# Attention and mixture-of-experts block on one core: a division without reciprocals, hidden tiles turned by DMA, down products three units late

## The reference

```python
def step(carry, kv_t):                     # over the 128 positions, per channel
    p, q, o = carry; kt, vt = kv_t
    no = maximum(o, u + kt); A = exp(o - no); E = exp(u + kt - no)
    y = (A * p + E * vt) / (A * q + E)
    no2 = maximum(w + o, kt); A2 = exp(w + o - no2); E2 = exp(kt - no2)
    return (A2 * p + E2 * vt, A2 * q + E2, no2), y
x = x + wkv(w, u, layernorm(x), ctx)       # k = layernorm(x), v = ctx
h = layernorm(x)
comb = top-2 of softmax(h @ gate_w.T), scattered to 8 columns
moe = sum_e comb[:, e] * ((silu(h @ eg[e].T) * (h @ eu[e].T)) @ ed[e].T)
sh  = sigmoid(h @ s_gate.T) * ((silu(h @ sg.T) * (h @ su.T)) @ sd.T)
out = x + moe + sh
```

## Time and profile before

| | us |
|---|---|
| median of 3 timed runs | 566.74 |
| lowest and highest of them | 566.08 and 566.8 |
| the profiled execution, whole | 566.06 |
| its span, first to last instruction | 564.3 |

### The profile page before, as it was taken

How to read it: one execution, slowest core, us unless ns; L and a number is a source line. 1 busy time by engine, 2 the same in 40 slices (tenths; PEclk the granted TensorE clock), 3 DMA queues, 4 the chain that set the end, 5 groups by cost and what they waited for, 6 DMA issues and landing times.

```text
span 564.3 us, 10142 instructions
## 1 busy us (share of the span) xinstructions
PE 486.2 (86%) x2671; PEld 258.5 (46%) x2671; DVE 421.3 (75%) x954; ACT 275.9 (49%) x534; POOL 345.4 (61%) x422
## 2 busy tenths in 40 slices
PE   1116789899999999999999979999999999999970
PEld 1113345345455555454555435445545555555530
DVE  5678987899989899999898867566656656666650
ACT  4848837575573864765837333433333333333310
POOL 5767956857948669588486364334375565555332
PEclk9999989999999999999999999999999999999995
DMA  7970105105213223151101320315576776677453
GB/s 283 415 271 19 38 19 187 57 21 188 76 46 143 77 82 143 38 188 62 52 20 39 105 88 15 113 45 102 101 122 117 141 119 116 110 131 123 69 73 38
DMA packets 25929, 59.14 MB, mean 105 GB/s; under 512 B 6314, under 2 KB 6314, under 8 KB 24338
## 3 DMA queue, kind: packets, MB, share of 16 engines
q0 software_dynamic: 9824, 20.90, 21.3%
q1 hardware_dynamic: 16050, 37.59, 18.5%
HBM read 37.83 MB, written 20.65 MB: 104 GB/s over the span
## 4 chain that ended last, share of the span: by engine, by line
PE 52%; POOL 17%; issue 10%; DVE 9%; DMA 7%; ACT 3%; SPq 1%; POOLq 0%; DVEq 0%; ACTq 0%
PE GU L884 28%; PE DN L899 14%; DMA out<-wall,idsa 5%; POOL wall L445 4%; PE XT L829 3%; PE HT L829 3%; POOL yb L429 2%; POOL nrm L411 2%; POOL nrm L413 2%; DVE wall L1071 2%; POOL wall L424 2%; POOL wall L421 2%; DVE wall L1078 1%; PE YT L829 1%; SPq L366 1%
## 5 line engine op out<-in xcount | busy, mean ns | idle before, releaser
L884 PE MATMUL GU<-wall,xt 128*128 128x512 f16 x768 | 187.0, 384 | 2.1 <-DVE wall L1173 2.0
L899 PE MATMUL DN<-wall,hx 128*128 128x512 f16 (+1 forms) x618 | 150.8, 380 | 7.2 <-DVE hx L1200 4.5
L884 PEld LDWEIGHTS GU<-wall,xt 128*128 128x128 f16 x768 | 74.8, 99 | 70.4 <-issue 3.7
L584 POOL DMA_INDIRECT out<-wall,idsa x39 | 62.0, 1590 | 73.1 <-SPq L370 35.1
L659 ACT ACTIVATE hx<-HT 128x256 f16<-128x256 f32 x103 | 39.0, 379 | 127.4 <-PE HT L829 110.6
L899 PEld LDWEIGHTS DN<-wall,hx 128*128 128x128 f16 x618 | 60.4, 98 | 81.9 <-issue 6.0
L1200 DVE TENSOR_TENSOR hx<-HT,hx 128x256 f16<-128x256 f32 x103 | 43.1, 418 | 64.3 <-ACT hx L659 59.7
L654 ACT ACTIVATE th<-GU,scl 128x256 f32<-128x256 f32 x103 | 48.5, 471 | 80.0 <-PE GU L884 76.1
L884 PE MATMUL GU<-wall,kb 128*128 x240 | 61.4, 379 | 0.2 <-DVE kb L1374 0.2
L884 PE MATMUL GU<-wall,xnb 128*128 x228 | 58.5, 379 | 0.6 <-DVE xnb L1374 0.6
L574 POOL DMA_INDIRECT xb<-xn_rows,idsi x39 | 40.2, 1030 | 30.5 <-DMA out<-xb 16.3
(11 more groups left out here) (163 smaller groups left out, 747.3 us busy)
## 6 DMA issues: line engine op xcount, KB each, us to landing
wall<-wgu SPq DMA_DIRECT2D x12, 1024.0 KB, 9.7
wall<-wd SPq DMA_DIRECT2D x12, 512.0 KB, 10.3
out<-xb SPq DMA_DIRECT2D x20, 256.0 KB
xb<-x SPq DMA_DIRECT2D x16, 256.0 KB, 2.7
cb<-ctx_t SPq DMA_DIRECT2D x16, 256.0 KB
xn_rows<-xnb SPq DMA_DIRECT2D x16, 256.0 KB
xb<-xn_rows,idsi POOLq DMA_INDIRECT x39
out<-wall,idsa POOLq DMA_INDIRECT x39
```

The costliest lines, as they stand in the source:

```text
L584: pool.indirect_dma_start(out, bass.IndirectOffsetOnAxis(ap=idsa[:, j:j + 1], axis=0), ye[j % RESULTS], None, compute_op=ALU.add).then_inc ...
L884: ins = nc.tensor.matmul(GU[par][:], lhs(xp, c), gate_up(base, wp, c), start=m == 0, stop=m == 3 * HC - 1)
L899: ins = nc.tensor.matmul(DN[:], hx[par][:, hp * IE + c * P:hp * IE + (c + 1) * P], down(base, wp, c), start=start and m == 0, stop=stop an ...
```

## The change

It has these parts:

- For tiles 3 to 15 (DIV = 3) the quotient is made without reciprocals. ScalarE takes an Exp of the denominator's bits read as an integer (`guess`), which is near the reciprocal; GpSimd multiplies denominator and numerator by it (`trial`); ScalarE takes two Squares (`correction`); VectorE multiplies in two passes (`divide`). The transposes YT of tile i move from the end of turn i to behind the first unit of turn i + 1.
- For the shared units the f32 transposes are gone. ScalarE and VectorE make the f16 halves of the hidden tile as it is, in hr (two buffers), and SP turns it into hx (three buffers, HX) by a DMA transpose of 128x512 f16. Routed units keep the f32 transposes, in the bank YT. The bank HT is named HB and holds one of the two hidden tiles.
- Down products come three units after their gate products, where they came two after. `accumulate` moves later in VectorE's order, `hidden_t` of the last routed unit moves ahead of the last down products, and GpSimd adds rows one slot later beside its gathers.
- Expert weights come in six DMAs of 256 KB, spread between the DMA transposes over two turns.
- The sums of squares of an expert are one matmul of four columns where they were two of two; VectorE adds them up.
- Some small index arrays move into space of a buffer that is free by then.

```diff
+HX = 3
+PIECES = 6
+DIV = LAG + 1
...
-        hb = [sb(f"hb{i}", [P, IE]) for i in range(2)]
-        hx = [sb(f"hx{i}", [P, 2 * IE], F16) for i in range(2)]
+        hb1 = sb("hb1", [P, IE])
+        hr = [sb(f"hr{i}", [P, 2 * IE], F16) for i in range(2)]
+        hx = [sb(f"hx{i}", [P, 2 * IE], F16) for i in range(HX)]
...
-        HT, DN = bank("HT"), bank("DN")
+        HB, DN = bank("HB"), bank("DN")
+        hb = [HB[:, 0:IE], hb1[:, :]]
+        hb_routed = [by_time[:, 0:IE], hb1[:, :]]
...
+            def turn_hidden(n):
+                sp.wait_ge(h_lo, n + 1)
+                wait_from(sp, dn, n - HX + 1)
+                sp.dma_start(hx[n % HX][:, :].rearrange("p (c t) -> p c t", t=P), hr[n % 2][:],
+                             transpose=True).then_inc(h_turned[n % HX], 16)
...
             def turn(i, j, sq_e, hi_e, ws_e, lo_e):
...
+                if j > 0:
+                    turn_hidden(n - 1)
+                if i == LAG:
+                    load_x(i + 3)
+                if i > LAG + 1 and i + 2 < B:
+                    load_x(i + 2)
+                if i < B - 1:
                     load_ctx(i + 1)
...
+                piece(0)
+                turn_hidden(n)
+                piece(1)
+                turn_hidden(n + 1)
+                store_xn(i - 1)
+                piece(2)
+                turn_hidden(n + 2)
+                if j > 0:
                     store_sum(j - 1)
...
+            def trial(t):
+                pool.wait_ge(guessed, t - DIV + 1)
+                nc.gpsimd.tensor_tensor(wkv(t, 2), wkv(t, 2), wkv(t, 0), ALU.mult).then_inc(tried, 1)
+                nc.gpsimd.tensor_tensor(wkv(t, 3), wkv(t, 3), wkv(t, 0), ALU.mult).then_inc(ymul, 1)
...
                 norm(i - 1, 1, agg2, norm2, xn_rdy)
                 if i == LAG:
                     shared_d_lo(1)
+                if i + 2 < B:
+                    norm(i + 2, 0, agg1, norm1, k_rdy)
+                if i >= DIV:
+                    trial(i)
                 if lo_e is not None:
                     expert_lo(lo_e, 2)
                 if ws_e:
                     expert_lo(ws_e, 0)
-                if i + 2 < B:
-                    norm(i + 2, 0, agg1, norm1, k_rdy)
...
-                quotient(i)
+                if i < DIV:
+                    quotient(i)
...
             for j in range(GATHERS, NSLOT):
                 gather_tile(j)
-                add_rows(j - GATHERS)
+                if j > GATHERS:
+                    add_rows(j - GATHERS - 1)
...
             def unit_hi(n, par):
...
+                act.wait_ge(h_rdy, n + 1)
+                if n >= 2:
+                    act.wait_ge(h_turned[(n - 2) % HX], 16 * ((n - 2) // HX + 1))
+                nc.scalar.activation(hr[par][:, 0:IE], hb[par], ACT.Copy).then_inc(h_hi, 1)
+
+            def guess(t):
+                act.wait_ge(nd, t + 1)
+                nc.scalar.activation(wkv(t, 0), wkv(t, 2).bitcast(I32), ACT.Exp, bias=divc[:, 0:1],
+                                     scale=GUESS_SCALE).then_inc(guessed, 1)
+
+            def correction(t):
+                act.wait_ge(tried, t - DIV + 1)
+                nc.scalar.activation(wkv(t, 1), wkv(t, 2), ACT.Square, bias=divc[:, 1:2],
+                                     scale=DIV_SCALE).then_inc(corrected, 1)
+                nc.scalar.activation(wkv(t, 2), wkv(t, 2), ACT.Square, bias=divc[:, 2:3],
+                                     scale=DIV_SCALE).then_inc(corrected, 1)
...
                 router_out(i - 2)
+                if i >= DIV:
+                    guess(i)
...
                 if i + 2 < B:
                     first_norm(i + 2)
+                if i >= DIV:
+                    correction(i)
                 unit_hi(n + 2, 0)
...
-                nc.tensor.matmul(LG[:, 0:2], ones[:], ssqe[:, 0:2], start=True, stop=False)
-                nc.tensor.matmul(LG[:, 0:2], ones[:], ssqe[:, 2:4], start=False, stop=True).then_inc(sq_sum, 1)
+                nc.tensor.matmul(LG[:, 0:4], ones[:], ssqe[:], start=True, stop=True).then_inc(sq_sum, 1)
...
                 if before is not None:
-                    down_products(n - 2, par, *before)
-                if not (isinstance(n, int) and n == 0):
-                    hidden_t(n - 1, 1 - par)
+                    down_products(n - HX, *before)
+                if n > N_EXP:
+                    hidden_t(n - 1)
...
                         router(i - 2, 2 + sum(a < i for a in SQUARED_IN))
+                        if i > LAG:
+                            y_back(i - 1)
                         if i + 1 < B:
                             keys_t(i + 1)
...
-                y_back(i)
...
-            down_products(n - 2, n % 2, base_of[NSLOT - 2], True, True, B + NSLOT - 2)
-            hidden_t(n - 1, (n - 1) % 2)
-            down_products(n - 1, (n - 1) % 2, base_of[NSLOT - 1], True, True, B + NSLOT - 1)
+            hidden_t(N_EXP + NSLOT - 1)
+            for j in range(NSLOT - HX, NSLOT):
+                down_products(N_EXP + j, base_of[j], True, True, B + j)
...
+            def divide(t):
+                dve.wait_ge(ymul, t + 1)
+                dve.wait_ge(corrected, (t - DIV) * 2 + 2)
+                STT(wkv(t, 3), wkv(t, 1), DIV_ADD[0], wkv(t, 3), ALU.add, ALU.mult).then_inc(half_div, 1)
+                dve.wait_ge(half_div, t - DIV + 1)
+                dve.wait_ge(y_t, t)
+                STT(grid(yb[:])[:, :, 1:T], grid(wkv(t, 2))[:, :, 1:T], DIV_ADD[1], grid(wkv(t, 3))[:, :, 1:T], ALU.add,
+                    ALU.mult).then_inc(y_rdy, 1)
...
                 hidden_lo(n + 2, 0)
+                if i >= DIV:
+                    divide(i)
                 hidden(n + 3, 1, SHARED)
...
-                if j == 1:
+                if j == HX - 1:
                     accumulate(B - 1)
-                if j >= 2:
-                    expert_rows(j - 2)
+                if j >= HX:
+                    expert_rows(j - HX)
                 hidden(N_EXP + j, r, expert_at[j])
```

More of the change, by code:

```diff
@@ L175, in build @@
         r_cmp, r_eid, r_row, r_one, r_of = taken(NSLOT * E), taken(NSLOT), taken(E), taken(E), taken(2)
+        eidi, idsi, idsa, wsl, pad_of = (taken(NSLOT) for _ in range(5))
+        eidi, idsi, idsa, before_i = (a.bitcast(I32) for a in (eidi, idsi, idsa, taken(RESULTS * NSLOT)))
         ids_back, ids_float = by_time[0:NSLOT, 0:P * LW].bitcast(I32), yb[0:NSLOT, 0:P]
@@ L328, in _ @@
             load_expert(0)
-            def turn(i, j, sq_e, hi_e, ws_e, lo_e):
-                if 0 < i < B - 1:
-                    load_ctx(i + 1)
-                if i == 1:
-                    load_expert(1)
-                if i + 1 in SQUARED_IN[2:]:
-                    load_expert(squares_of(i + 1))
-                if i > 0:
-                    store_xn(i - 1)
-                if j is not None and j > 0:
+            for i in range(LAG):
+                if i > 0:
+                    load_ctx(i + 1)
+                    load_expert(1)
+                    store_xn(i - 1)
+                load_x(i + 3)
@@ L340, in turn @@
                     store_sum(j - 1)
-                if i + 3 < B:
-                    load_x(i + 3)
                 if i == B - 1:
                     store_probs(0, 0, PART)
-            turns(turn)
+            turns(turn, LAG)
+            n = SU * (B - LAG)
+            turn_hidden(n - 1)
             sp.wait_ge(y_rdy, B)
-            load_expert(E - 1)
+            sp.wait_ge(y_first, B - DIV)
+            load_expert(E - 1, 0, 3)
+            turn_hidden(n)
             store_xn(B - 1)
+            load_expert(E - 1, 3, 6)
@@ L351, in _ @@
+            turn_hidden(n + 1)
+            turn_hidden(n + 2)
             store_sum(B - LAG - 1)
+            turn_hidden(n + 3)
             store_probs(1, PART, B)
-            for j in range(B - LAG, B - 1):
-                store_sum(j)
+            for u in range(3):
+                turn_hidden(n + SU + u)
+            store_sum(B - 2)
+            turn_hidden(N_EXP - 1)
             store_sum(B - 1)
@@ L391, in other_consts @@
             def other_consts():
+                for k, value in enumerate((GUESS_BIAS, *DIV_BIAS)):
+                    link(pool.memset(divc[:, k:k + 1], value))
                 link(pool.memset(all16[:], 1.0))
@@ L590, in _ @@
                 gather_tile(j)
[L591 to L592 removed]
+                if j > GATHERS:
+                    add_rows(j - GATHERS - 1)
+            for j in range(NSLOT - GATHERS - 1, NSLOT):
                 add_rows(j)
@@ L1282, in turn @@
                     keys(i + 1)
-                reciprocals(i, 1, 2)
+                if i < DIV:
+                    reciprocals(i, 1, 1)
+                if later:
+                    accumulate(j - 1)
+                if i < DIV:
+                    reciprocals(i, 2, 1)
                 hidden_lo(n + 1, 1)
-                reciprocals(i, 3, 1)
+                if i < DIV:
+                    reciprocals(i, 3, 1)
                 hidden(n + 2, 0, SHARED)
@@ L1389, in _ @@
```

(5 more changed lines are left out.)

122 lines of the change are left out of this document (73 added, 49 removed).

## The result

The changed kernel takes **576.22 us** (median of 4 runs, 574.28 to 578.52) beside 566.77 (566.08 to 567.41) of the kernel before: ratio 1.017, 95% interval 1.012 to 1.021. It is slower by some 9.5 us. The forecast was 549.2, the range 544 to 568.

A forecast was written before the change was run, and what follows sets the result against it. The prediction took TensorE, busy 98% of the shared expert's turns, as the bound, with VectorE almost as full. Gains of 23.4 us less losses of 6.5 gave net 16.9: 566.06 - 16.9 = 549.2 us, range 544 to 568.

The forecast's parts named there:

- Hidden transposes, their DMAs: Shared units: dropping TensorE's f32 transposes gains 12.6 us; the DMA transposes replacing them land in 3.5 us, unseen.
- the second estimate: DMA transposes of hidden tiles: 5.2 us each, from the Trainium skill's 1309 ns per 128x128 block; kernel some 650 us.
- Rival 3: Slower: in the turns the transposes hold the DMA engines or land late; 567 to 620 us, chance 0.18.
- The waits at YT, HT and for low halves (6.2): TensorE's waits in the turns at these three places go, gaining 6.2 us.
- the price of the new waits: In the turns, XT comes late through GpSimd's longer queue: 0.15 us a turn taken, 2 us lost.
- VectorE's share falls to some 80% of a shorter turn: In the turns the division takes 2.3 us off VectorE, which lets TensorE keep its gain.
- Rival 2: A ring of the side engines sets the turn, giving back 4 to 12 us: 553 to 562 us, chance 0.22.
- Start: At the kernel's start, some TensorE waits for YT, HT and down products leave: 0 to 6 us gained, 3 taken.
- Tail: At the kernel's end, slot 36's rows are weighed later, behind the last hidden transposes: 4.1 us lost.
- Gather of slot 5: The gather of slot 5's rows goes out later behind accumulate(15) and lands late: 0.4 us lost (0 to 2.5).
- Sum: Whole kernel: 23.4 us gained, 6.5 lost, net 16.9, giving 549.2 us.

The follow-up runs named there:

- e7: The changed kernel with GpSimd's low halves of experts 1 to 6 cut to 8 columns, that part of the result left out: 547.28 us.
- e1: The changed kernel with the division undone: all 16 tiles take the four reciprocals and GpSimd's one product: 561.14 us.
- e12: The kernel before with the division without reciprocals alone, hidden tiles still turned on TensorE, YT at the turn's end: 582.33 us.
- e6: The changed kernel with both untransposed hidden tiles of the shared units in the PSUM bank HB: 573.5 us.
- e9: e6 with GpSimd's norm of the tile put ahead of the second low half of the expert's weights: 572.5 us.
- e11: e7 with seven more products of 8 columns after each cut product, and both hidden tiles in PSUM: 560.28 us.
- e10: The changed kernel with the reciprocals back, both hidden tiles in PSUM and GpSimd's norm ahead of the second low half: 550.65 us.
- e14: The changed kernel with VectorE's small steps moved from ahead of the divide to the turn's end: 594.61 us.
- e8: The changed kernel with reciprocals back and both hidden tiles in PSUM, each DMA transpose done twice, the second after the first lands: 624.38 us.

## Why the prediction was wrong, step by step

- **Hidden transposes, their DMAs**: right. The landing was taken as 3.5 us (5.2 in the second estimate) and is 2.4 at the median; nothing in the changed kernel waits for it. e7's two turns, 35.29 us, are inside 35.0 to 35.4. Rival 3 had the time of the result but not its cause; e1 and e7, with all transposes, are faster than before.
- **The waits at YT, HT and for low halves (6.2)**: right only in e7. In the changed kernel YT waits 8.2, for VectorE now.
- **The step that failed: the price of the new waits, "between 0 and 0.9 us a turn; I take 0.15"**, as the sum has it (2.0 us). Two turns take 40.2 us where 35.0 to 35.4 were forecast, 2.5 us more a turn, nearly three times the upper bound; over the twelve tiles it is the 27 us by which e7 is ahead. TensorE waits 26 us, at XT, GU and YT. The working took each duration from a row and let it stand. But VectorE's durations depend on what GpSimd does beside it, and GpSimd's on VectorE. In the turn shown, the small steps meet three products instead of one and wait 2.8 us, on a ring of in-order queues. The earlier trace rows could not show the price: before, that ring had slack behind TensorE. The trace of before did have the sign of it, 366 ns as the mean for a step that takes 0.16 us at its shortest.
- **"VectorE's share falls to some 80% of a shorter turn"** failed as well, and its sum is off: 92% of 18.9 us less 2.3 are 15.2 us, 80% of the old turn but 86% of one of 17.6. It came to 89% of a longer turn. Yet it did not decide: e7 has the forecast turn with VectorE at 93%, and e12 loses 17 us with VectorE at 82%.
- **Rival 2** (a ring of the side engines) is nearest to what happened; its price, 4 to 12 us given back, was too small: 27 came. It counted GpSimd's busy time and not what GpSimd and VectorE do to each other. Its shares (nearly 90% for GpSimd) did not come either: the ring closes with every engine below 90%.
- **Start**: 3 us taken, 5.7 measured, near the bound of 6. **Tail**: 4.1 forecast; the rows of slot 36 start 3.63 us after the last tanh (552.76 and 549.13) where they started 0.27 ahead of it, 3.9. **Gather of slot 5**: TensorE waits 0.9 us for it, 0.4 was taken.
- **Sum**: forecast 549.2; e7 is at 547.3. That the sum comes so near is in part luck: the start gave 2.7 us more than was taken, and the small terms were not measured one by one. The 29 us from there to the changed kernel come with GpSimd's wide low halves, 7 of them with reciprocals too.

What stays open: how the 22 us of interaction divide between stretched steps and held queues. e6 gives 3 us and e9 1 more, at a lower clock; e11 lies 13 us from e6 and from e7, but changes the phase as well. They don't add to a full account. The best kernel that computes everything is e10, with the reciprocals, the tile in PSUM and the norm first: 550.65, 2.5% less than before (0.970 to 0.979), some 14 us.

## What to carry to other kernels

Before moving work from one kind of instruction to another on VectorE, look at what GpSimd runs beside it, and at the mean against the shortest duration of the smallest steps of both: the step over 16 columns had a mean of 366 ns and a shortest of 160 in the kernel before, so it was waiting, though it counts as busy. An engine that is freed brings nothing if its work lies on a ring of in-order queues; walk the chain of the new order once around and put every wait and every stretched step on it. And moving the stretched steps away, as in e14, can cost more than they do, if another queue waits for them.

## What the runs showed of the hardware

- A VectorE instruction whose operands lie in SBUF can last as long as the GpSimd product that runs when it starts (0.85, 1.25 and 1.18 us for steps of 0.15), the product itself keeping its 1.27; a pass of 0.68 that starts with 0.88 of a product left takes 1.43. Putting one of the operands in PSUM brought 888 ns back to 396 and the kernel 6 us.
- The later one waits on GpSimd too: its products on f32 tiles take 1.45 to 1.47 us instead of 1.27, 11 times of 26 in the changed kernel, where a low half of the SBUF tile runs when they start, and 1.72 in e14 behind a pass of the divide.
- An indirect DMA of GpSimd takes 0.96 us by itself, and 1.33 and 1.62 when a VectorE pass with two SBUF inputs has 0.38 and 0.62 us left at its start. Such a pass that starts beside an indirect DMA keeps its 0.69 us; a conversion over two columns (posi) took 0.40 there instead of 0.16.
- A step need not get in between two products: in e11 one lasted 2.43 us and ended, at 225.46, with the second of two (225.43).
- A DMA transpose of 128x512 f16 within SBUF lands 2.4 us after its issue at the median of e8 and holds SP for 1.19 us at its issue, in some cases 2.1. Four a turn raise the share of the DMA engines from 0.29 and 0.21 to 0.46 and 0.33.
